# Edge loop of a graph layer: TensorE alternates second layer and sum, VectorE works two tiles ahead, twelve row buffers

## The reference

```python
h = shifted_softplus(f_ij @ Wf1 + bf1)
W = (h @ Wf2 + bf2) * rcut_ij[:, None]
m_s = s2 * W[:, :2 * F]
m_v = (v2.reshape(e, 2 * F, 3) * W[:, 2 * F:4 * F, None]).reshape(e, 6 * F)
x_ij = jnp.concatenate([m_s, m_v, m_w, m_t], axis=1)
agg = jax.ops.segment_sum(x_ij, idx_i, num_segments=n)
S = agg[:, :2 * F] @ (W1_s / np.sqrt(2 * F))
V = jnp.einsum('nmi,mc->nci', agg[:, 2 * F:8 * F].reshape(n, 2 * F, 3), W1_v) / np.sqrt(2 * F)
```

## Time and profile before

| | |
|---|---|
| time, median of 3 runs | 1663.13 us (1662.01 to 1665.01) |
| the profiled execution: time / span | 1661.82 / 1660.1 us |
| mean granted TensorE clock | 0.965 |
| TensorE matmuls busy | 1366.3 us, 82% |
| VectorE busy | 1068.0 us, 64% |
| ScalarE busy | 826.0 us, 50% |
| GpSimd busy | 797.8 us, 48% |
| GpSimd row gathers (L563) | 342, mean 945 ns |
| GpSimd record gathers (L552) | 342, mean 945 ns |

### The profile page before, as it was taken

One profiled execution on the slowest core, in us unless ns is written; L12 is line 12 of the kernel. 1 busy time (PEld: TensorE's weight loads), 2 busy tenths in 40 slices (PEclk: granted clock), 3 DMA queues, 4 the chain that ended last, 5 costly groups with the idle time before them and its releaser, 6 DMA issues. The chain is left out here.

```text
span 1660.1 us, 26803 instructions
## 1 busy us (share of the span) xinstructions
PE 1366.3 (82%) x7054; PEld 776.0 (47%) x7054; DVE 1068.0 (64%) x2530; ACT 826.0 (50%) x2145; POOL 797.8 (48%) x844
## 2 busy tenths in 40 slices
PE   0777688888888888888888888888899269999997
PEld 0552344444444444444444444444458146555554
DVE  6899567777777777777777777777787731111110
ACT  3679646556556556565565565565565201111111
POOL 2257556656656656666566566566550012222111
PEclk9999799999999999999999999999999569999999
DMA  5044133334333333333333333333342314554531
GB/s 218 1 191 128 37 88 91 104 99 106 103 86 106 94 96 105 107 104 111 104 100 94 88 88 94 87 91 91 87 106 89 130 57 142 168 179 144 148 81 20
DMA packets 65670, 172.66 MB, mean 104 GB/s; under 512 B 13963, under 2 KB 22523, under 8 KB 64989
## 3 DMA queue, kind: packets, MB, share of 16 engines
q0 software_dynamic: 43424, 105.53, 24.7%
q1 hardware_dynamic: 22196, 66.57, 11.2%
HBM read 148.72 MB, written 18.08 MB: 100 GB/s over the span
## 5 line engine op out<-in xcount | busy, mean ns | idle before, releaser
L1096 PE MATMUL PS<-prod,oneh 128*64 128x256 f32 x2052 | 508.4, 389 | 122.1 <-DVE region_s L920 87.2
L563 POOL DMA_INDIRECT gath<-table_d,recs x342 | 323.1, 945 | 307.1 <-PE PS L1089 211.8
L1096 PEld LDWEIGHTS PS<-prod,oneh 128*64 128x64 f32 x2052 | 259.7, 138 | 362.4 <-DVE prod L908 135.6
L1089 PE MATMUL PS<-prod,oneh 128*64 128x256 f32 x1368 | 375.7, 395 | 28.3 <-issue 26.9
L552 POOL DMA_INDIRECT recs<-rec_d,inv_i x342 | 323.1, 945 | 117.1 <-issue 116.5
L1077 PE MATMUL PS<-wf_sb,h_t 128*128 128x512 f32 x684 | 335.0, 613 | 2.9 <-issue 2.9
L908 DVE TENSOR_TENSOR prod<-PS,gath 128x768 f32<-128x768 f32 x342 | 324.1, 948 | 0.0
L684 ACT ACTIVATE oneh<-oneh,recs 128x64 f32<-128x64 f32 x1026 | 272.7, 336 | 77.6 <-issue 40.1
L906 DVE TENSOR_TENSOR prod<-PS,gath 128x256 f32<-128x256 f32 x342 | 143.8, 421 | 201.3 <-remote 152.5
L920 DVE TENSOR_TENSOR region_s<-region_s,PS 128x512 f32 x342 | 233.4, 683 | 44.3 <-issue 33.7
L669 ACT ACTIVATE soft<-PS,b1col 128x512 f32<-128x512 f32 x86 | 59.1, 687 | 322.0 <-remote 314.1
(11 more groups left out here) (270 smaller groups left out, 1481.8 us busy)
## 6 DMA issues: line engine op xcount, KB each, us to landing
region_r<-wu SPq DMA_DIRECT2D x16, 512.0 KB
region_r<-wd SPq DMA_DIRECT2D x16, 512.0 KB
region_u<-wu SPq DMA_DIRECT2D x16, 512.0 KB, 4.3
region_u<-wd SPq DMA_DIRECT2D x16, 512.0 KB, 5.4
recs<-rec_d,inv_i POOLq DMA_INDIRECT x342
gath<-table_d,recs POOLq DMA_INDIRECT x342
region_u<-rec_in SPq DMA_DIRECT2D x1, 5168.0 KB, 17.4
rec_d<-region_u SPq DMA_DIRECT2D x1, 5168.0 KB
```

The costliest lines, as they stand in the source:

```text
L563: nc.gpsimd.indirect_dma_start(out=gath[:, t % GRING, :], out_offset=None, in_=table_d, in_offset=bass.IndirectOffsetOnAxis(ap=recs[:, q % ...
L1089: return nc.tensor.matmul(PS[0:WIDE, bank, half * 2 * FDIM:(half + 1) * 2 * FDIM], oneh[:, slot, 0, :], prod[:, slot, 2 * half:2 * half + ...
L1096: return nc.tensor.matmul(to, oneh[:, slot, 1 + i, :], prod[:, slot, P_Q:P_B + i + 1:1 + i, :], start=i == 0, stop=i == 2, skip_group_chec ...
```

## The change

The row buffers become a ring of twelve (`rows`), placed in `region_u`, where the unsorted edges were. The row gather waits for the products of tile t-12 and no longer for the sum of tile t-6. How far records run ahead (AHEAD = 6) stays.

TensorE takes in each step the second layer of tile t+4, then the sum of tile t; the first layer of quad q+2 comes in the second step of quad q, ahead of that step's second layer. VectorE takes in step t: flush of t-1, one-hot of t+3, products of t+2, with the transpose in the quad's first step and `hidden` of quad q+2 at the end of its fourth. ScalarE takes the seed of t+5 and the scaled one-hots of t+2, with the soft-plus operations of quad q+2 at the head of the third step. Before the loop stand the second layers of four tiles, the first layers of two quads, and the products of two tiles. The parameter `left` goes; `tiles_of(q)` and `there(t)` take its place.

```diff
-GRING = 6
+GRING = QUAD * RING
+AHEAD = 6
@@ GpSimd
                     if t >= GRING:
-                        hold(pool, s_done, 2 * (t - GRING + 1), pool_passed)
+                        hold(pool, prod_ready, t - GRING + 1, pool_passed)
                     nc.gpsimd.indirect_dma_start(
-                        out=gath[:, t % GRING, :], out_offset=None, in_=table_d,
+                        out=rows[:, t % GRING, :], out_offset=None, in_=table_d,
@@ ScalarE
+                    for k in range(tiles_of(q)):
+                        t = QUAD * q + k
+                        if k == 2 and there(t + 6):
+                            size_of_z(q + 2)
+                            exp_of_z(q + 2)
+                            log_of_z(q + 2)
+                        if there(t + 5):
+                            seed(t + 5, (k + 1) % QUAD)
+                        if there(t + 2):
+                            scaled_one_hots(t + 2, (r + (k + 2) // QUAD) % RING, (k + 2) % QUAD)
@@ VectorE
+                    for k in range(tiles_of(q)):
+                        t = QUAD * q + k
+                        if not isinstance(t, int) or t >= 1:
+                            flush(t - 1, SUM_BANKS[(QUAD * r + k - 1) % SRING], first=isinstance(t, int) and t == 1)
+                        if there(t + 3):
+                            at, on = (r + (k + 3) // QUAD) % RING, (r + (k + 3) // QUAD) // RING
+                            one_hot(t + 3, at, (k + 3) % QUAD, (k + 3) % QUAD, body + on, first=isinstance(t, int) and t < 1,
+                                    n=tiles_of(q + (k + 3) // QUAD))
+                        if k == 0 and there(t + 8):
+                            transpose_records((r + 2) % RING, body + (r + 2) // RING, n=tiles_of(q + 2))
+                        if there(t + 2):
+                            at, on = (r + (k + 2) // QUAD) % RING, (r + (k + 2) // QUAD) // RING
+                            products(t + 2, at, (k + 2) % QUAD, (k + 2) % QUAD, body + on)
+                        if k == 3 and there(t + 5):
+                            hidden(q + 2, (r + 2) % RING)
@@ TensorE
-                    for k in range(here):
-                        second_layer(q, r, k, k)
-                        if k == 2 and left >= 1:
-                            first_layer(q + 1, (r + 1) % RING)
-                    for k in range(here):
-                        sum_tile(QUAD * q + k, k, SUM_BANKS[(QUAD * r + k) % SRING],
-                                 first=isinstance(q, int) and q == 0 and k < SRING)
+                    for k in range(tiles_of(q)):
+                        t = QUAD * q + k
+                        if k == 1 and there(t + 7):
+                            first_layer(q + 2, (r + 2) % RING)
+                        if there(t + 4):
+                            second_layer(q + 1, (r + 1) % RING, k)
+                        sum_tile(t, k, SUM_BANKS[(QUAD * r + k) % SRING], first=isinstance(t, int) and t < SRING)
```

More of the change, by code:

```diff
@@ L66, in scalars_until, with tiles_of, there @@
     return sum(by_scalar(c) for c in range(n))
-def tiles_of(left):
-    return QUAD if left >= 1 else LAST
+def tiles_of(q):
+    return LAST if isinstance(q, int) and q == QUADS - 1 else QUAD
+def there(t):
+    return not isinstance(t, int) or t < USED
 def column(n):
@@ L714, in _ @@
                 log_of_z(0, first=True)
+                scaled_one_hots(0, 0, 0)
+                scaled_one_hots(1, 0, 1)
+                size_of_z(1)
+                exp_of_z(1)
+                log_of_z(1)
+                seed(4, 0)
                 for r in range(RING):
-                    step(r, r, first=r == 0)
+                    step(r, r)
                 with act.Fori(1, BODIES) as i:
@@ L720, in _ @@
                 for q in range(BODIES * RING, QUADS):
-                    step(q, q % RING, left=QUADS - 1 - q)
+                    step(q, q % RING)
             @block.vector
@@ L955, in _ @@
                 transpose_records(1, 0)
+                products(0, 0, 0, 0, 0)
+                products(1, 0, 1, 1, 0)
+                hidden(1, 1)
                 for r in range(RING):
-                    step(r, r, 0, first=r == 0)
+                    step(r, r, 0)
                 with dve.Fori(1, BODIES) as i:
@@ L961, in _ @@
                 for q in range(BODIES * RING, QUADS):
-                    step(q, q % RING, q // RING, left=QUADS - 1 - q)
-                flush_of(QUADS - 1, (QUADS - 1) % RING, LAST - 1)
+                    step(q, q % RING, q // RING)
+                flush(USED - 1, SUM_BANKS[(USED - 1) % SRING])
             @block.tensor
```

82 lines of the change are left out of this document (24 added, 58 removed).

## The result

The changed kernel takes 1802.74 us (median of 4 runs, 1794.08 to 1806.11), the kernel before 1664.07 us beside it (4 runs, 1662.01 to 1668.94): a ratio of 1.0821, interval 1.0774 to 1.0868. The forecast was 1726 with a range up to 1795. The sign and, in the main, the mechanism it named are those of the trace, the size is 77 us short and the time lies 8 us outside the range.

What follows compares the result with a forecast made beforehand. It took the loop as bound by GpSimd's gather bursts plus pauses while TensorE's completions are held. At five tiles between pauses, 3.28 - 3.095 = 0.185 us per tile x 342 = +63; 1663 + 63 = 1726 us, range 1528 to 1795.

Steps and rivals of the forecast that it cites:

- The hold: Edge loop: TensorE's completions are held during GpSimd's gather bursts, released 2.71 us after the last gather's start; chance 0.5.
- The restart behind VectorE: GpSimd after a release: waits for VectorE's flush, one-hot and two products, 2.45 us in place of 0.93.
- the formula: GpSimd's cycle in the edge loop: (2n - 1) x 1.25 + 2.71 + 2.45 = 2.5 n + 3.9 us.
- n: Tiles between GpSimd's pauses in the edge loop: taken as 5, giving 3.28 us per tile.
- the tiles started under the hold: TensorE in the edge loop: work started while completions are held, about 66 instructions, 2.4 tiles.
- The prompt time: TensorE between release and next hold: 6.5 to 8.5 us after the change, 2.5 to 3.3 tiles.
- The end of the range: Upper end of the forecast time: 1795 us, with n = 4 at 1793; above 1793 chance 0.04.
- The rival without a hold: TensorE's completions not held in the edge loop: 10.9 us per quad, 1536 us, or 1490 with hidden not late; chance 0.34.
- The wait for hidden: TensorE's next second layer waits for VectorE's hidden operation: 10.9 us per quad, against 10.37 were hidden not late.
- TensorE's step: TensorE per tile: second layer 0.96 plus sum 1.41, 2.37 us; with the first layer's 0.89, 10.37 us per quad.
- The sign of that rival: Whole kernel without held completions: called faster, 127 us less, from 12.38 to 10.9 us per quad.
- VectorE and ScalarE: Edge loop: VectorE 9.1 us per quad, under TensorE and GpSimd; ScalarE no new work, stays hidden, nothing.

Runs made afterwards that it cites:

- the ring alone: Kernel before with only the ring of twelve row buffers, released by the products, old engine order: 1464.09 us (1.0003) on chip C, 1856.87 us (1.1031) on chip B.
- the run that removes it: Kernel after with VectorE's hidden operation ahead of the flush in every fourth step: 1538.3 us, ratio 1.0522, beside 1587.17 us for the kernel after.

## Why the prediction was wrong, step by step

**The hold.** That TensorE's completions are held and come 2.71 after GpSimd's last gather, and that the change keeps this state, is what the trace of after shows in the burst printed above (2.73, 2.74) and in over half of its late releases. Shown on chips like that one; on three others it doesn't exist for either kernel (for the kernel before this is read from its time and from the trace of the ring alone). The prediction had "no row shows the mechanism", and that remains: the experiments show that gathers back to back are not sufficient and that the release can come inside a burst. Whether on a held chip it is GpSimd's issuing or the traffic of its gathers that goes with the hold was not tested: the rows went by SyncE on a prompt chip only. The 1055 us that the prediction gives for the loop is a slip, 86 x 12.39 = 1066; nothing was built on it.

**The restart behind VectorE** is the price named, 2.45 in place of 0.93, and it is 2.89 in the burst shown, 0.44 more: the product that releases it ends at 625.08 (624.13 + 0.95), and GpSimd starts 0.78 later, where 0.30 stood. Over all 59 long stops, though, GpSimd stands 3.92 us, less than the 2.71 + 2.45 - 0.94 = 4.22 of the formula.

**The failing step is n.** "I take n = 5": in the trace 46 of 58 stretches between long stops have eight gathers, n = 4, as before. The formula at n = 4 gave 1793 us, and the profiled execution took 1794. That the two agree so closely is in part luck. The mean of 8.8 gathers is n = 4.4, which gives 13.5 us a quad by the formula; the shorter stops make it 13.80, with quads from 11.7 to 16.6. And the loop grew by 121.7 us, not 130; 10.5 us came ahead of the first flush, where the prediction had "0 to 3 us once, taken as nothing". Of the two parts of n, the tiles started under the hold came out right: between the first layer at 618.00 and the release TensorE started two tiles, where 2.4 stood. The prompt time had the right length too, 6.5 to 8.5 us forecast, 8.0 from the release at 610.01 to 618.00. Its lower end was misread, though. The rows named for it, from 607.00 to 610.48 and to 614.2, span 3.5 to 7.2 us, not 5 to 7; so read, the count is 4.3 to 5.7 tiles for the change, and 3.7 to 5.2 for the kernel before, where 4 is seen. And the prompt time was filled at 2.6 us a tile, TensorE's own pace, for 2.5 to 3.3 tiles. TensorE made two: at 612.56 it had waited 1.53 for a seed and at 615.51 0.39 for hidden. Seeds and hidden hang on products that VectorE could only begin after the release, the very lateness that the sum had charged to GpSimd alone. Of the prediction's own count, too, the half tile by which it came out high on the kernel before should have been taken off: 4.4 to 5.2, and then n = 4 would have had more of the chance.

**The end of the range** was n = 4 at its mean, 1793, and 2 us. Nothing was left for the scatter of such a loop, in which the four runs lie from 1794 to 1806, nor for the late start of the loop, 10.5 us, nor for the restart's own uncertainty: half a microsecond more in each of 86 pauses is 43 us.

**The rival without a hold** was put at 1536 and 1490. The prompt chips run it: 1587 for the kernel after, 1538 with hidden no longer late. Its 10.9 a quad was too small by 0.6. The wait for hidden is there, as worked out (10.9 - 10.37 = 0.53 forecast, 0.55 in the timeline, 49 us by the run that removes it). The mis-sized term is TensorE's step: 2.37 came from rows in which the second layer stood behind the first layer, which needs no change on the way in. Between two sums it takes 1.06, not 0.96, the sum 1.44, not 1.41, and the first layer behind a sum 1.00, not 0.89: 3 x 1.06 + 0.95 + 4 x 1.44 + 1.00 = 10.89, against 10.87 measured. The sentence that the drain is within the rows, whatever it costs, was the error: it was within them in one direction only.

**The sign of that rival** was a second error. It was called faster by setting a loop without the hold against the kernel before with it. Where there is no hold, the kernel before has none either: 1463, a quad of 10.0 set by GpSimd. The change is 8.6% slower there. What was left for the 0.34 of this rival was that the change itself would end a hold that is there, and on the held chips the hold shows in every kernel with the new order.

**VectorE and ScalarE** as costed: nothing of their own work shows. That the flush, now first in a step, stops VectorE under the hold was said, and it is the 205.9 us in the waits of after, with 52.2 and 44.1 more under other releasers.

## What to carry to other kernels

A deeper ring whose release goes through another engine can be slower than a short one that is released by the completion itself: look at what the releasing engine must do after the event that everybody waits for. When a stall is suspected to vanish, cost the old kernel without the stall too, before calling the new one faster. And take the price of a matmul between two of another kind from a row that has the change on both sides; here it is 0.34 us for there and back. A sum that closes on one burst is not yet a rule for the loop: count the bursts that keep to it.

## What the runs showed of the hardware

One and the same kernel took 1462.8 to 1463.8 us on three chips, and 1664, 1683 and 1689 us elsewhere: a difference of 14 to 15%, and no lower clock explains it (0.965 and 0.958 in the profiles of the kernel before on held chips, 0.964 in that of the ring alone on chip C). It lies in the edge loop: 86 quads of 12.4 to 12.7 us against 10.0, the latter read from the ring alone, which took the same time as the kernel before. On each of the five chips the 7 to 13 runs of the kernel before that stand beside the experiments agree within 0.6% (the profiled one on B took 1692.74 us, 0.6% above their median), so this is a property of the chip or of its state over minutes; which of the two can't be told, since no chip came twice in the five groups, and that of the result is not on record. That a loss of 8 to 9% has two different causes on the two sorts of chip was not expected, and neither could have been seen from one of them alone.
